# Convolution weights loaded behind image 0's second piece, and image 0's scale finished by VectorE

## What is computed

```python
x = x + _L0_conv_ref(_gn(x), w0, b0)      # 3x3 convolution, 8 -> 8 channels
x = x + _L1_conv_ref(_gn(x), w1, b1)      # the same
x = x + _L2_conv_ref(_gn(x), ...)         # per channel: 256 -> 1024, gelu, 1024 -> 256
x = x + _L3_conv_ref(_gn(x), w3, b3)      # 3x3 convolution again
def _gn(v, G=4, eps=1e-05): ...           # (g - mean) / sqrt(var + eps) by group
```

## Time and profile before

| | |
|---|---|
| median of 3 runs | 554.52 us (551.06 to 556.36) |
| profiled execution, its own time | 555.89 us |
| its span, first to last instruction | 554.10 us |
| mean granted TensorE clock | 0.987 |
| busy: TensorE, VectorE, ScalarE, GpSimd | 514.6, 371.7, 295.3, 170.3 us |

### The profile page before, as it was taken

How to read it: one execution, slowest core, us unless ns; L and a number is a source line. 1 busy time by engine, 2 the same in 40 slices (tenths; PEclk the granted TensorE clock), 3 DMA queues, 4 the chain that set the end, 5 groups by cost and what they waited for, 6 DMA issues and landing times.

```text
span 554.1 us, 9155 instructions
## 1 busy us (share of the span) xinstructions
PE 514.6 (93%) x3374; PEld 258.0 (47%) x3374; DVE 371.7 (67%) x637; ACT 295.3 (53%) x363; POOL 170.3 (31%) x188
## 2 busy tenths in 40 slices
PE   0689999996989999999999999999999999999976
PEld 0444445563544444444444444444444446675422
DVE  4899999987966395095094094094185479989633
ACT  2899988553734453353353353353345574898440
POOL 4699888887460000000000000000000000399440
PEclk9899999998999999999999999999999999999998
DMA  8855555543020222022022022022023220036795
GB/s 321 352 137 151 139 135 143 130 124 153 0 77 1 76 76 77 0 76 76 0 76 76 0 76 76 0 76 76 1 86 142 76 77 1 3 97 192 243 310 219
DMA packets 13880, 57.41 MB, mean 104 GB/s; under 512 B 3084, under 2 KB 3212, under 8 KB 10764
## 3 DMA queue, kind: packets, MB, share of 16 engines
q1 hardware_dynamic: 12444, 53.23, 29.9%
q10 hardware_dynamic: 1404, 3.74, 2.0%
HBM read 30.03 MB, written 8.39 MB: 69 GB/s over the span
## 4 chain that ended last, share of the span: by engine, by line
PE 62%; DVE 20%; POOL 4%; DMA 4%; ACT 3%; issue 3%; SPq 2%; DVEq 0%; POOLq 0%; ACTq 0%
PE PS L1090 26%; PE PS L1116 26%; DVE ST L707 7%; DVE X L746 6%; PE PS L992 4%; DMA X<-x 3%; PE PS L985 2%; DVE X L764 2%; POOL XN L397 2%; SPq L263 2%; PE PS L1047 2%; DVE SM L722 1%; PE PS L1146 1%; DMA HALO<-XN 1%; ACT SCR L550 1%
## 5 line engine op out<-in xcount | busy, mean ns | idle before, releaser
L1090 PE MATMUL PS<-XT,W1S 128*128 (+1 forms) x768 | 171.6, 382 | 2.8 <-POOL XT L446 2.5
L1116 PE MATMUL PS<-HID,W2S 128*128 128x512 f16 x720 | 159.5, 379 | 1.6 <-DVE W2S L771 1.6
L550 ACT ACTIVATE SCR<-PS,CONST 128x512 f32<-128x512 f32 x128 | 87.1, 686 | 64.6 <-PE PS L1090 27.8
L1090 PEld LDWEIGHTS PS<-XT,W1S 128*128 128x128 f16 x768 | 75.6, 99 | 92.0 <-issue 5.7
L1116 PEld LDWEIGHTS PS<-HID,W2S 128*128 128x128 f16 x720 | 70.3, 98 | 83.0 <-issue 1.8
L397 POOL TENSOR_TENSOR XN<-SCR,XN 128x1024 f16<-128x1024 f32 (+1 forms) x61 | 100.3, 1671 | 13.8 <-ACT SCR L509 13.5
L771 DVE SCALAR_TENSOR_TENSOR W2S<-W2F,W2S 128x2048 f16<-128x2048 f32 x10 | 22.9, 2291 | 114.3 <-ACT W2S L546 114.3
L374 POOL MEMSET XN<- 128x128 f16 x6 | 2.8, 462 | 303.0 <-PE PS L1116 302.7
L707 DVE BATCH_NORM_STATS2 ST<-X 128x6 f32<-128x512 f32 x128 | 81.4, 680 | 9.3 <-DMA X<-x 8.1
L504 ACT ACTIVATE XN<-X,SC 128x1024 f16<-128x1024 f32 (+1 forms) x61 | 64.1, 1050 | 20.1 <-POOL SC L388 18.6
L746 DVE SCALAR_TENSOR_TENSOR X<-PS,X 128x512 f32<-128x512 f32 x96 | 59.8, 680 | 21.4 <-PE PS L1007 21.3
(11 more groups left out here) (52 smaller groups left out, 478.8 us busy)
## 6 DMA issues: line engine op xcount, KB each, us to landing
W1F<-w SPq DMA_DIRECT2D x10, 1024.0 KB, 4.8
W2F<-w SPq DMA_DIRECT2D x10, 1024.0 KB, 4.8
HALO<-XN SPq DMA_DIRECT2D x48, 129.9 KB
HALO<-XN SPq DMA_DIRECT2D x48, 121.8 KB
out<-X SPq DMA_DIRECT2D x11, 512.0 KB, 4.5
X<-x SPq DMA_DIRECT2D x2, 2048.0 KB, 18.9
HALO<-XN SPq DMA_DIRECT2D x40, 64.9 KB
HALO<-XN SPq DMA_DIRECT2D x40, 60.9 KB
```

The lines of the kernel that those rows point to most:

```text
L550: act.activation(SCR[:, ft % 2, 0:CH], bank(ft % G_RING), ACT.Gelu, bias=BT[:, ds(e * FT + ft, 1)], scale=1.0 / (XS * WS)).then_inc(gelu_o ...
L1090: mm = pe.matmul(bank(ft % G_RING), W1S[:, w, h * NF + ft * P:h * NF + (ft + 1) * P], rhs, start=(n == 0), stop=(n == 3 * DH - 1))
L1116: mm = pe.matmul(bank(G2_BANK + h), W2S[:, w, ft * NW + h * P:ft * NW + (h + 1) * P], HID[slot][:, part, ft], start=(ft == 0 and part == 0 ...
```

## The change

ScalarE's queue issues CONST, then waits for HALF and loads the activation table, then waits for image 0's second piece, and only then issues CWF and the ones. GpSimd's `scale_and_bias(0)` ends after the power; a new function on VectorE, `first_scale`, does the other three instructions of image 0, behind `variance(0)` and ahead of image 1's statistics.

```diff
@@ -379,6 +379,9 @@
             r0, t = RS[:, 0:1], RS[:, 1:2]
 
             pool.tensor_tensor(r0, SM[:, n, 2:3], HALF, ALU.pow).then_inc(rstd_ok, 1)
+            if n == 0:
+
+                return
             pool.wait_ge(rstd_ok, RSTD_STEPS * n + 1)
             pool.tensor_scalar(t, r0, r0, SM[:, n, 4:5], ALU.mult, ALU.mult).then_inc(rstd_ok, 1)
             pool.wait_ge(rstd_ok, RSTD_STEPS * n + 2)
@@ -489,13 +492,15 @@
     @block.scalar
     def _(act):
         act.dma_start(CONST[:], consts).then_inc(cst_in, 16)
+        act.wait_ge(half_ok, 1)
+        act.activation(RS[:, 3:4], HALF, ACT.Gelu)
+
+        act.wait_ge(x0_in[1], 16)
         act.dma_start(CWF[:].rearrange("p l k -> p (l k)"), cw).then_inc(cw_in, 16)
         for s in range(SLOTS):
             rows = HALO[s][HK:HK + HALF_P + 1:HALF_P, 0].rearrange("p t j -> p (t j)")
             act.wait_ge(zero_ok[s], 2)
             act.dma_start(rows, ones).then_inc(ones_in[s], 16)
-        act.wait_ge(half_ok, 1)
-        act.activation(RS[:, 3:4], HALF, ACT.Gelu)
 
         def normalise_piece(m):
             g, i, n = PIECES[m]
@@ -730,6 +735,18 @@
             dve.tensor_scalar(SM[:, n, 4:5], stat_psum(n, 1), EPS, -0.5 * XS, ALU.add, ALU.mult
                               ).then_inc(var_ok, 1)
 
+        def first_scale():
+
+            r0, t = RS[:, 0:1], RS[:, 1:2]
+            dve.wait_ge(rstd_ok, 1)
+            dve.tensor_scalar(t, r0, r0, SM[:, 0, 4:5], ALU.mult, ALU.mult).then_inc(rstd_ok, 1)
+            dve.wait_ge(rstd_ok, 2)
+            dve.tensor_scalar(SC[:, 0, 0:1], t, 1.5 * XS, r0, ALU.add, ALU.mult
+                              ).then_inc(rstd_ok, 1)
+            dve.wait_ge(rstd_ok, 3)
+            dve.tensor_tensor(SC[:, 0, 1:2], SM[:, 0, 3:4], SC[:, 0, 0:1], ALU.mult
+                              ).then_inc(norm_ok, 1)
+
         def input_stats(b, i):
             if b == 0:
                 if i in X0_CUTS:
@@ -776,6 +793,7 @@
         aggregate(0)
         deviation(0)
         variance(0)
+        first_scale()
         for i in range(NCH):
             input_stats(1, i)
         aggregate(1)
```

## The result

The changed kernel takes 559.66 us in the median of 10 runs (557.68 to 563.95), the kernel before 554.74 us (551.06 to 558.90) beside it. The ratio is 1.009 with a 95% interval of 1.0058 to 1.0123: slower by some 5 us, where I had forecast no change, at 554.7 us, and a range up to 558.0. The ratios of this document leave out the executions that lie over 1.5% above the fastest of their kernel, among them one of 690.12 us in e5. The profiled execution took 561.36 us, its span is 559.5 us and its mean granted clock 0.975. In the changed kernel VectorE's spread L722 is line L727, the low part L397 is L400, the weights' low part L422 is L425, the warm-up matmuls L1177 are L1195.

The account below looks back on a forecast made before the run. A chain of waits from image 2's load was taken to bound the start, with image 0's scale close beside it. Power +0.6 us and scale quicker by 0.45 us gave d = +0.2 us, median 554.7 us, range 551.8 to 558.0 us.

Parts of the forecast that it names:

- The views and the chain: Start of kernel: small shifts of image 0's first rounding, either way, move everything behind by about as much.
- d: Shift of image 0's first rounding on ScalarE, 16.35 us before; forecast +0.2 us, bounds -0.65 to +1.6 us.
- The landing of the weights: CWF, issued at 7.2 us behind image 0's second piece, lands at 11.8 us, bounds 10.9 to 12.8 us.
- the estimate of 2.9 us: Weights' transfer alone, by the skill's 2.0 us plus bytes at 436 GB/s; would land at 10.1 us; not used.
- L422 ahead of the power: GpSimd's queue: image 0's power waits for the weights' low part until 15.2 us instead of 14.58, +0.6 us.
- The gain of the images' transfers: Image 0's last piece lands at 10.7 instead of 11.2 us, so its variance is ready 0.5 us earlier.
- The collision of L422 with L722: If GpSimd's L422 starts first, VectorE's spread of image 0 is held until its end, power 1.0 to 1.2 us after.
- The scale on VectorE: Image 0's three one-column instructions moved off GpSimd: power to first rounding 1.3 instead of 1.77 us, gaining 0.45 us.
- The table's load and the ones: ScalarE's queue: earlier GELU table load and later loads of ones cost nothing, the ones with 4 us of cover.
- Weights late: Rival: image 1's packets hold the weights, power waits until 16.2 us, d +1.2 to +1.6 us, 556 us; chance 0.13.
- The fourth: Rival: second piece lands near 8 us, nothing freed for images, variance stays at 14.5 us; counted in the late case.
- The third, TensorE's clock: Rival: a pause drops TensorE's clock before the tiles at 32.18 us, 1.4 us; with late weights 557.5 us; chance 0.05.

Follow-up runs that it names:

- e5: The whole change run again unaltered, against the kernel before: ratio 1.0067, first rounding at 20.08 us.
- e1: Kernel before with only the three one-column instructions of image 0's scale moved to VectorE, weights' load left in place: ratio 1.0026.
- e8: Kernel before, but only the first convolution's weights loaded at the start, the others behind step 1's halo transfers: ratio 0.9992 to before.
- e9: Kernel before with only the first convolution's weights loaded at the start and image 0's scale finished on VectorE: ratio 1.0021 to before.
- e10: Whole change without the wait for image 0's second piece; weights issued at 1.24 us: ratio 1.0017 to before.
- e12: Unaltered repeat of e8 (first convolution's weights alone at the start): ratio 1.0017 to before.
- e11: Whole change, with SyncE issuing images 1, 2 and 3 only once the weights have landed: ratio 1.0015 to before.
- e2: Whole change with only the later weights' load kept; image 0's scale back wholly on GpSimd: ratio 1.0065 to before.
- e7: Whole change with image 0's power ahead of the weights' low part in GpSimd's queue: ratio 1.0042 to before.
- e13: Kernel before plus twelve dummy matmuls in TensorE's waits between group mean and variance of images 1 and 2: ratio 0.9961.
- e3: Whole change with 18 instead of 8 warm-up dummy matmuls on TensorE at the start: ratio 1.0078 to before.
- e14: Whole change with 18 warm-up matmuls and twelve dummy matmuls in the waits of images 1 and 2: ratio 1.0058 to before.
- e15: Kernel with the first convolution's weights alone at the start, plus twelve dummy matmuls in the waits of images 1 and 2: ratio 0.9985 to before.
- e6: Whole change with image 1 loaded in four transfers instead of two and image 2 in four instead of one: ratio 1.0058 to before.

## Why the prediction was wrong

**The views and the chain.** Half right. That a later first rounding goes through to the end about one for one is borne out: the eight measurements with d between 2.2 and 3.9 us have ratios from 1.0042 to 1.0090, that is 2.3 to 5.0 us. But the prediction said it of both directions. The five measurements with all images issued at the start and no dummies that have the rounding 0.4 to 0.85 us earlier (e1, e8, e9, e10, e12) lie from 0.9992 to 1.0026, four of them above 1. None alone says much, but together they show no gain. And the earlier trace rows, from which I took that no idle place is left, ends at 130 us: the last wait near 540 us, with its 1.13 to 4.06 us, lies behind it.

**The landing of the weights is the step that failed.** I bounded it by 10.9 and 12.8 us and took 11.8; it was 15.2. Two terms were too small. The first packets were to follow the issue by 1.0 to 1.5 us, from a row at 2.2 us, when the images' own first packets were only starting. With the images issued it took 3.2 us, in which 1.39 MB of images moved, and e11 shows that this is their doing, as it falls to about 1 us without images 1 to 3 ahead. And 128 pairs of packets were to take 2.3 to 3.5 us; they took from 10.4 to about 14.8, 4.4 us. There the upper bound had the mechanism and about the size of a packet (7.3 KB; 7.7 measured), and too few of them: 194 image packets moved in that time, not 128, 1.9 MB in all with the weights. The sum 7.18 + 3.2 + 4.4 + 0.4 gives the 15.2 us. With the landing 3.4 us later than I took it, the power came at 18.55 us and not at 15.2, and d was +3.6 us and not +0.2. That the transfer took 7.6 us from issue in the earlier trace rows stood in my text, and 7.2 + 7.6 = 14.8 us would have been the nearest row. I set those 7.6 us against the estimate of 2.9 us, and then summed packets without asking where they had gone.

**L422 ahead of the power** held: 1.75 us from the first copy to L425, and the power at its end, 18.55 us. The gain of the images' transfers was there too (variance 1.2 us earlier, not 0.5), and found no use, as GpSimd wasn't free for the power. The collision of L422 with L722 was not met in the change. It was met in e11, with the price foreseen: VectorE's spread of image 0 lasts until the low part's end, 1.56 us for 0.22. The rule of the Trainium skill, "SBUF — State Buffer", section "SBUF: two separate sides", that the one who starts first keeps the shared ports for its whole instruction, holds there. By the Trainium skill, "DMA: Bandwidth & Descriptors", section "Anatomy of one DMA", I had an estimate of 2.9 us for the weights alone; e11 has 3.1 us with only image 0's rest beside them, near that estimate, and the whole change 8.0 us. That figure of the Trainium skill is for one transfer on another path and leaves out what is queued ahead.

**The scale on VectorE** was to gain 0.45 us and gained 0.34 (1.43 us against 1.77). Its halt was 5.8 us, where 15.2 + 0.56 + 0.1 - 14.0 = 1.9 us were foreseen. It is not shown to cost anything, and the reason given fits: GpSimd's third low part, from 25.26 to 27.32 us, holds image 1's spread anyway, and e2 and e7, without the halt, are no faster than their rounding says.

**The table's load and the ones** are not shown to cost anything, as foreseen: e10, with both moved, has 1.0017 with 1 inside the interval.

**The rivals.** "Weights late" was the right one, with 0.13, but sized at +1.2 to +1.6 us where +3.6 came. The fourth, that the change frees nothing for the images, is wrong. The third, TensorE's clock, exists: e12, and the changed kernel's first profile, show image 2's spread missing its slot, TensorE's pause of some 2 us and slow first tiles, which e8 and e5 of the same two kernels do not have. It needed no late weights. Whether before has it too is open: e13 keeps the clock up and gains 0.4%, 2.2 us, but its profile differs from before's in the last wait alone. How much of the changed kernel's loss beyond d is the clock stays open: e3 moved the pause and not the time, and e14 didn't hold the clock. The two measured ratios, 1.0090 and 1.0067, give a loss of 3.7 to 5.0 us for a d of 3.6, so the rest may be nothing.

## What to carry to other kernels

Here a small transfer that joined while larger ones were issued waited twice, 3.2 us for what was already ahead and then 4.4 us packet by packet beside it. Price such a transfer from a row with the same traffic ahead, or issue it first. Look at what stands behind its consumer in an in-order queue: here the power waited 5.2 us for weights that it does not use. Where TensorE's clock falls in a pause that another engine's wait makes, other executions may fall differently, so a single profile can mislead by some us, at the start and at the end. A few dummy matmuls in such pauses are worth a try: they gained 0.4% in e13 and nothing that can be told in e15.

## What the runs showed of the hardware

With the images issued, the first packet of ScalarE's queue moved 3.2 us behind its issue in the changed kernel and 3.7 us in e6; with only image 0's rest ahead, about 1 us. ScalarE's queue issued a transfer at 1.24 us, 0.07 us behind the start of a table load of 1.28 us and ahead of its end (e10). VectorE's three-operand instruction on one column, started 0.08 us behind a GpSimd subtraction, lasted 1.56 us instead of 0.22 (e11). One program's first update of X moved by 3.0 us between two profiles, with TensorE's clock (e8, e12). The last wait for halos' transfers took between 1.13 us (e6) and 4.06 us (before), and after the 4.06 us the tiles ran at the 1.2 GHz level, 0.63 us each instead of 0.38. In e2 the granted clock read 1.00 where seven matmuls took 3.15 us.
